# A ring of six buffers with exponents a batch ahead, and the last multiplication of each weight unit on GpSimd

## What is computed

```python
x = x + mlstm(layernorm(x), ctx, ctx, Wi, bi, Wf, bf, ln_scale)   # 16 heads of 32
x = x + ffn(layernorm(x), w_gate, w_up, w_down)                   # 512 -> 2048 -> 512
# mlstm, per batch and head, s = 256:
log_D = where(ltr, fcum_i - fcum_j, -inf) + ig_j
D     = exp(log_D - rowmax(log_D))
C     = (q @ k.T / sqrt(32)) * D
h     = (C / (max(|C.sum(-1)|, exp(-rowmax)) + 1e-6)) @ v          # then layernorm per head, scaled
# ffn: every operand is quantized in blocks of 32 along its last axis
mx_linear(x, w) = q_act(x) @ q_w(w).T
out   = mx_linear(silu(mx_linear(x, w_gate)) * mx_linear(x, w_up), w_down)
```

## Time and profile before

| | us |
|---|---|
| median of 3 runs | 636.48 |
| lowest and highest | 633.6 and 640.59 |
| the profiled execution, its own time | 635.27 |
| its span, first to last instruction | 633.5 |
| busy: TensorE, VectorE, ScalarE, GpSimd | 519.4, 453.5, 247.2, 208.0 |
| mean granted TensorE clock, share of full | 0.732 |

### The profile page before, as it was taken

The page is one execution under the profiler, slowest core; times in us unless marked ns, Lnnn a source line. Parts: engine busy times, 40 slices in busy tenths (PEclk is TensorE's granted clock), DMA queues, the critical chain, the costliest instruction groups (busy, mean ns, idle before and its releaser), DMA issues.

```text
span 633.5 us, 10373 instructions
## 1 busy us (share of the span) xinstructions
PE 519.4 (82%) x3465; PEld 355.1 (56%) x3465; DVE 453.5 (72%) x639; ACT 247.2 (39%) x343; POOL 208.0 (33%) x207
## 2 busy tenths in 40 slices
PE   2699984989859698597895986855999999999994
PEld 2599973767646466475574764622444444444441
DVE  3899995566657867578566775469788888888781
ACT  1566642242324425233334342242443343344331
POOL 3222001101515316152171331435434444443542
PEclk9966855575557657555565565677999999999998
DMA  6654414111221402214032020201011121020010
GB/s 198 210 205 147 128 58 128 57 55 50 73 65 34 138 21 82 67 34 137 0 100 70 1 67 0 67 0 66 2 57 43 33 66 34 33 66 33 33 66 33
DMA packets 30564, 43.70 MB, mean 69 GB/s; under 512 B 6980, under 2 KB 11972, under 8 KB 30532
## 3 DMA queue, kind: packets, MB, share of 16 engines
q1 hardware_dynamic: 30532, 43.26, 21.4%
HBM read 34.41 MB, written 8.85 MB: 68 GB/s over the span
## 4 chain that ended last, share of the span: by engine, by line
PE 36%; DVE 32%; issue 18%; POOL 8%; ACT 4%; DMA 1%; DVEq 1%; POOLq 1%; SPq 0%; ACTq 0%
PE psA L1256 10%; PE psA L1330 5%; PE psA L1339 5%; POOL kTa L666 5%; PE psB L1247 3%; DVE qTa L1112 3%; DVE kTa L1103 3%; DVE pam L917 3%; PE psC L1213 3%; DVE wq L943 3%; DVE wy L940 3%; PE psB L1245 2%; DVE wam L917 2%; DVE wm L935 2%; PE psB L1349 2%
## 5 line engine op out<-in xcount | busy, mean ns | idle before, releaser
L1256 PE MATMUL psA<-vp,CT 128*128 128x33 f32 x512 | 107.2, 370 | 50.0 <-DVE CT L1016 49.9
L1256 PEld LDWEIGHTS psA<-vp,CT 128*128 128x128 f32 x512 | 100.5, 293 | 68.4 <-issue 64.3
L1016 DVE SCALAR_TENSOR_TENSOR CT<-psA,Dt 128x512 f32<-128x512 f32 x64 | 42.7, 688 | 95.4 <-ACT Dt L793 87.8
L666 POOL TENSOR_TENSOR kTa<-kTa,ps 128x1024 bf16<-128x1024 bf16 x32 | 61.2, 1913 | 103.7 <-DVE kTa L1115 103.7
L793 ACT ACTIVATE Dt<-psB 128x512 f32<-128x512 f32 x64 | 37.3, 594 | 91.4 <-PE psB L1247 91.4
L1330 PE MATMUL psA<-WgT,qTa 128*128 128x512 bf16 x256 | 65.2, 401 | 7.4 <-ACT qTa L821 4.3
L1357 PE MATMUL psC<-WdT,kTa 128*128 128x512 bf16 x256 | 61.9, 386 | 2.4 <-ACT kTa L869 2.4
L1339 PE MATMUL psA<-WuT,qTa 128*128 128x512 bf16 x256 | 60.9, 381 | 0.0
L869 ACT ACTIVATE kTa<-psB 128x1024 bf16<-128x1024 bf16 x32 | 32.8, 1024 | 55.2 <-PE psB L1349 54.7
L1103 DVE TENSOR_TENSOR kTa<-kTa,psA 128x1024 f32<-128x1024 f32 x32 | 39.0, 1220 | 18.7 <-PE psA L1339 18.5
L713 ACT ACTIVATE wm<-wm,wbase 128x1024 f32<-128x1024 f32 x24 | 27.6, 1149 | 58.5 <-DVE wm L935 58.5
(11 more groups left out here) (131 smaller groups left out, 923.5 us busy)
## 6 DMA issues: line engine op xcount, KB each, us to landing
early<-in_x_dram SPq DMA_DIRECT2D x16, 512.0 KB, 4.1
early<-in_ctx_dram SPq DMA_DIRECT2D x8, 512.0 KB, 4.6
wraw<-in_L_ffn_w_down_dram SPq DMA_DIRECT2D x8, 512.0 KB, 5.9
...
```

The costliest lines, as they stand in the source:

```text
L666: nc.gpsimd.tensor_tensor(blocks(pd[h]), blocks(pc[h]), spread(ps4[h][:, :], PB), ALU.mult).then_inc(pq_ready.sem, 1)
L1016: nc.vector.scalar_tensor_tensor(out=CT[n % HPC][:, :], in0=psA[:, n % HPC, :], scalar=float(DH) ** -0.5, in1=Dt[n % 2][:, :], op0=ALU.mul ...
L1256: last = nc.tensor.matmul(psA[:, j, i4 * VW:(i4 + 1) * VW], CT[n % HPC][:, i4 * P:(i4 + 1) * P], vp[p][:, c, HPC * i4 + j, :], start=i4 == ...
```

## The change

- `Dt` (2 buffers) and `CT` (4) become one ring `DC` of 6. `c_mult` writes its product over the exponents that it read, so `exps` no longer waits for `c_ready`, nor `c_mult` for `h_done`.
- Decay and `exps` 0 to 3 of batch b + 1 run at the end of step b; `centre(b, 1)`, `copy_v(b, 1)`, `state(b)` and `copy_state(b)` move from step b - 1 into step b. TensorE starts a step with a `w_transpose`, then heads 0 to 3 with nothing between them. ScalarE runs `x1_norm` ahead of `copy_h(b, 1)`, and `round_const(2b + B + 3, 1)` stays last.
- `w_back` moves from VectorE to GpSimd, in the preparation and in the steps. In a step GpSimd runs `head_rsqrt`, `residual`, `carry_q`, `w_back`, `x1_rsqrt`, `w_back`, `weigh`, `back_x`. Two waits are added on VectorE: `w_front` waits for the `w_back` of two units before (it overwrites `ws4`), `w_pow` for the `w_round` of the unit before.
- SyncE issues `load_carry(b + 1)` ahead of the wait for `state_mm` and of `load_ctc(b + 1)`.

The diff, cut to its core (what is left out renames the buffers, deletes `w_back` from VectorE's list and brings the first batch's order in line):

```diff
@@ -179,17 +180,16 @@
         Sst = [sb(f"Sst{p}", [P, HC, VW]) for p in range(2)]
         vp = [sb(f"vp{p}", [P, NCH, NH, VW]) for p in range(2)]
         vw = sb("vw", [P, NH, VW])
-        Dt = [sb(f"Dt{n}", [P, HC * P]) for n in range(2)]
-        CT = [sb(f"CT{n}", [P, HC * P]) for n in range(HPC)]
+        DC = [sb(f"DC{n}", [P, HC * P]) for n in range(DCN)]
         hf = [sb(f"hf{p}", [P, NCH, NH, VW]) for p in range(2)]
...
@@ -485,12 +485,12 @@
                 sp.wait_ge(d_mm.sem, d_mm.at(b, 1))
                 settle(sp)
                 load_decay(b + 1, 1 - p)
+                sp.wait_ge(qs_ready.sem, qs_ready.at(b, 1))
+                settle(sp)
+                load_carry(b + 1)
                 sp.wait_ge(state_mm.sem, state_mm.at(b, 1))
                 settle(sp)
                 load_ctc(b + 1)
-                sp.wait_ge(qs_ready.sem, qs_ready.at(b, 1))
-                settle(sp)
-                load_carry(b + 1)
                 if weights:
                     sp.wait_ge(y_ready.sem, y_ready.unit(2 * b + B + 2))
                     settle(sp)
...
@@ -552,6 +552,12 @@
                 chain.link(nc.gpsimd.tensor_scalar(tmp, src, 1.0, LN_EPS, ALU.mult, ALU.add))
                 chain.link(nc.gpsimd.tensor_tensor(dst, tmp, mhalf[:, 0:NCH], ALU.pow))
                 return nc.gpsimd.tensor_tensor(bias, negmean, dst, ALU.mult)
+
+            def w_back(w, p):
+                gp.wait_ge(wn_ready.sem, wn_ready.unit(w))
+                settle(gp)
+                nc.gpsimd.tensor_tensor(blocks(wq[p][:, :]), blocks(wq[p][:, :]), spread(ws4[p][:, :], UB),
+                                        ALU.mult).then_inc(wq_ready.sem, 1)
 
             def x_rsqrt(b):
                 gp.wait_ge(mv_ready.sem, mv_ready.at(b, 1))
...
@@ -584,6 +590,8 @@
             def pre_step(b, p, n, first, last):
                 if not last:
                     x_rsqrt(b + 1)
+                if not first:
+                    w_back(b - 1, 1 - p)
 
             x_rsqrt(0)
             tables()
...
@@ -647,14 +655,19 @@
                 if not first:
                     residual(b - 1)
                 if not last:
+                    carry_q(b + 1, 1 - p)
+                w_back(2 * b + B + 1, 1)
+                if not first:
+                    x1_rsqrt(b - 1)
+                if not last:
+                    w_back(2 * b + B + 2, 0)
                     weigh(b + 1, 1 - p)
-                    carry_q(b + 1, 1 - p)
-                if not first:
-                    x1_rsqrt(b - 1)
                 if not first:
                     back_x(b - 1)
 
+            w_back(B - 1, 1)
             weigh(0, 0)
+            w_back(B, 0)
             carry_q(0, 0)
             pipeline(ch, gp, step)
 
...
@@ -788,9 +800,8 @@
                                      ACT.Copy, scale=float(DH) ** -0.5).then_inc(state_ev.sem, 1)
 
             def exps(b, n):
-                act.wait_ge(c_ready.sem, c_ready.at(b, max(n - 1, 0)))
                 act.wait_ge(d_mm.sem, d_mm.at(b, n + 1))
-                nc.scalar.activation(Dt[n % 2][:, :], psB[n % 2][:, :], ACT.Exp).then_inc(d_exp.sem, 1)
+                nc.scalar.activation(DC[n % DCN][:, :], psB[n % 2][:, :], ACT.Exp).then_inc(d_exp.sem, 1)
 
             def copy_h(b, p, c):
                 if c == 0 and not (isinstance(b, int) and b < 2):
...
@@ -821,38 +832,37 @@
                 nc.scalar.activation(spent_b[:, b, 0:NCH * E], psC[1][:, :].bitcast(BF16), ACT.Copy).then_inc(xqT_ev.sem, 1)
 
             def step(b, p, n, first, last):
-                exps(b, 0)
-                exps(b, 1)
-                exps(b, 2)
-                exps(b, 3)
+                evac_gate_up(2 * b + B, 0, b)
+                if not first:
+                    head_power(b - 1)
+                copy_h(b, p, 0)
                 exps(b, 4)
-                copy_h(b, p, 0)
                 exps(b, 5)
-                if not first:
-                    head_power(b - 1)
-                if not last:
-                    copy_v(b + 1, 1 - p, 0)
-                evac_gate_up(2 * b + B, 0, b)
+                copy_v(b, p, 1)
                 if not first and not (isinstance(b, int) and b == 1):
                     evac_xq(b - 2)
-                if not last:
-                    copy_v(b + 1, 1 - p, 1)
+                copy_state(b, p)
                 exps(b, 6)
                 exps(b, 7)
                 if not last:
                     round_const(2 * b + B + 2, 0)
+                if not first:
+                    x1_norm(b - 1)
                 copy_h(b, p, 1)
-                if not first:
-                    x1_norm(b - 1)
+                evac_gate_up(2 * b + B + 1, 1, b)
+                if not last:
+                    exps(b + 1, 0)
+                    exps(b + 1, 1)
+                    copy_v(b + 1, 1 - p, 0)
+                    exps(b + 1, 2)
+                    exps(b + 1, 3)
                 square(b, p)
                 if not last:
-                    copy_state(b + 1, 1 - p)
-                evac_gate_up(2 * b + B + 1, 1, b)
-                if not last:
                     round_const(2 * b + B + 3, 1)
 
-            copy_state(0, 0)
             round_const(B + 1, 1)
+            for k in range(HPC):
+                exps(0, k)
             pipeline2(ch, act, step)
             head_power(B - 1)
 
...
@@ -925,6 +935,7 @@
             def w_front(w, p, n):
                 ve.wait_ge(w_ld[p], 16 * n + 16)
                 ch.link(reduce_blocks(blocks(wraw[p][:, :]), wam[p][:, :]))
+                ve.wait_ge(wq_ready.sem, wq_ready.unit_before(w, 2))
                 ch.link(power(wam[p][:, :], ws4[p][:, :]))
                 ch.link(inverse(ws4[p][:, :], winv[p][:, :], INV_W))
                 nc.vector.tensor_tensor(blocks(wy[p][:, :]), blocks(wraw[p][:, :]), spread(winv[p][:, :], UB),
...
@@ -932,6 +943,7 @@
 
             def w_pow(w, p):
                 ve.wait_ge(y_ready.sem, y_ready.unit(w))
+                ve.wait_ge(wn_ready.sem, wn_ready.unit_before(w, 1))
                 nc.vector.tensor_scalar(wm[:, :].bitcast(I32), wy[p][:, :].bitcast(I32), EXPO, None,
                                         ALU.bitwise_and).then_inc(pow_ready.sem, 1)
 
...
@@ -1004,17 +1009,15 @@
                                     ALU.subtract).then_inc(split_ready, 1)
 
             w_round(B, 0)
-            w_back(B, 0)
             w_pow(B + 1, 1)
 
             ch = Chain(ve, dve_step, 2 * DVE_LINKS)
 
             def c_mult(b, n):
                 ve.wait_ge(qk_done.sem, qk_done.at(b, n + 1))
-                ve.wait_ge(h_done.sem, h_done.at(b, max(n - HPC + 1, 0)))
                 ve.wait_ge(d_exp.sem, d_exp.at(b, n + 1))
-                nc.vector.scalar_tensor_tensor(out=CT[n % HPC][:, :], in0=psA[:, n % HPC, :], scalar=float(DH) ** -0.5,
-                                               in1=Dt[n % 2][:, :], op0=ALU.mult, op1=ALU.mult).then_inc(c_ready.sem, 1)
+                nc.vector.scalar_tensor_tensor(out=DC[n % DCN][:, :], in0=psA[:, n % HPC, :], scalar=float(DH) ** -0.5,
+                                               in1=DC[n % DCN][:, :], op0=ALU.mult, op1=ALU.mult).then_inc(c_ready.sem, 1)
 
             def head_var(b, p):
                 n = hf[p][:, :, :, DH]
...
@@ -1074,7 +1077,6 @@
                 w_round(2 * b + B + 1, 1)
                 if not first:
                     head_norm(b - 1, 1 - p)
-                w_back(2 * b + B + 1, 1)
                 for k in range(HPC, 2 * HPC):
                     c_mult(b, k)
                 if not last:
...
@@ -1084,7 +1086,6 @@
                 if not last:
                     w_front(2 * b + B + 3, 1, b + B // 2 + 1)
                     w_round(2 * b + B + 2, 0)
-                    w_back(2 * b + B + 2, 0)
                 if not first:
                     x1_round(b - 1)
                 if not last:
...
@@ -1274,51 +1275,50 @@
                     last = nc.tensor.transpose(dst[:, k * P:(k + 1) * P], xd[:, k * P:(k + 1) * P], identb[:, :])
                 last.then_inc(xqT_mm.sem, 1)
 
+            def decay_qk(b, p):
+                decay(b, p, 0)
+                qk(b, 0)
+                decay(b, p, 1)
+
             def step(b, p, n, first, last):
+                w_transpose(2 * b + B, 0, rows_order)
                 for k in range(HPC):
                     heads(b, p, k)
-                    decay(b, p, k + 2)
-                if not last:
-                    centre(b + 1, 0)
+                decay(b, p, 4)
+                decay(b, p, 5)
+                centre(b, 1)
                 qk(b, 1)
-                w_transpose(2 * b + B, 0, rows_order)
                 if b >= 2:
                     pe.wait_ge(wT_ev.sem, wT_ev.unit(2 * b + B))
                     x_transpose(b - 2)
-                if not last:
-                    centre(b + 1, 1)
-                heads(b, p, 4)
+                state(b)
                 decay(b, p, 6)
-                heads(b, p, 5)
                 decay(b, p, 7)
```

(21 more changed lines are left out.)

26 lines of the change are left out of this document (10 added, 16 removed).

## The result

The changed kernel takes 567.06 us (median of 4 runs, 564.68 to 572.07) against 635.04 for the kernel before (4 runs). The ratio is 0.8947, interval 0.890 to 0.899: 68 us less, where 584 had been forecast and 562 to 609 given as the range. The profiled execution took 566.52 us, its span is 564.7 against 633.5. Some kernels have executions over 1.5% longer than their fastest; the ratios here leave these out and the medians take them in, and the profiles of e2, e7 and e10 fell on such a one.

The account below looks back on a forecast made before the run. A loop of about 25 us of TensorE's list, 13.5 of VectorE's and 2.6 of handing over bounds the attention steps. 635.3 less 49.9 (six steps), 1 (ends) and 0 (preparation) gives 584 us, range 562 to 609.

Parts of the forecast that it names:

- rival B: Attention steps: TensorE at the upper clock level throughout, so VectorE bounds at 29.0 us a step; 560 us total, chance 0.09.
- A full step: Attention step on TensorE: 35.8 of work less 5.5 for the clock plus 2 of waiting, 32.3 us.
- the clock term: TensorE's time at the upper clock level in a step: 5.5 us taken, bounds 3.3 and 10.3.
- The ends of the stage: Attention stage's ends: +3.2 ahead of heads(0, 0), -3 in step 0, -1 in the last step; together -1 us.
- `w_back` off VectorE: Attention steps: two w_back of 1.22 us leave VectorE's list; port lock costs 0 to 3.8 a step, 1 taken.
- The added waits: Attention steps: w_front waits 0 to 1 us, w_pow nothing, TensorE for copy_h 0 to 3, 2 taken.
- The preparation: Before the attention steps: eight w_back leave VectorE but TensorE doesn't get shorter; 0 us, bounds -1.5 and +1.5.
- The signs: New profile: steps of 31 to 34 us, c_mult right behind w_pow, TensorE waiting for hf, clock 0.55 to 0.65.
- A: Attention steps: clock stays as it is, waits at their bounds, 35.5 us a step; 604 us total, chance 0.2.
- D: Attention steps: VectorE and GpSimd exclude each other throughout, 45.3 us a step; slower at 663 us, chance 0.04.
- E: Attention steps: exps still last in the loop, only 2.4 + 1 us a step go; 615 us, chance 0.03.
- C: Attention steps: next exponents late, copy_h(b, 1) held another 4 us, 36.3 us a step; 608 us total, chance 0.08.

Follow-up runs that it names:

- e2: Kernel before with every w_back moved to GpSimd, nothing else changed; 626.55 us, ratio 0.986.
- e7: Changed kernel with copy_h(b, 1) ahead of x1_norm and eight added matmuls, results unused, ahead of heads 0; 560.90 us, ratio 0.882.
- e10: Changed kernel with copy_h first, x1_round behind c_mult 0 to 3 of a later step and eight matmuls added before heads 0; 570.41 us, ratio 0.895.
- e1: Changed kernel with every w_back back on VectorE, ring and early exponents kept; 574.45 us, ratio 0.906.
- e8: Kernel before with the ring of six buffers and without the waits for c_ready and h_done, all orders kept; 632.98 us, ratio 0.996.
- e5: Changed kernel with the w_back of the preparation (7 of its 8) on VectorE again; 567.70 us, ratio 0.899.
- e4: Changed kernel with copy_h(b, 1) ahead of x1_norm(b - 1) on ScalarE; 569.85 us, ratio 0.897.
- e12: Repeat run: changed kernel with copy_h(b, 1) ahead of x1_norm and eight added matmuls ahead of heads 0; 563.26 us, ratio 0.881.

## Why the prediction was right, point by point

*The time.* The measured 567.06 lies within 562 to 609, but 17 us below the 584 that was forecast and 7 below the band of 574 to 594 that was given 0.56. It is nearer rival B's 560 than the forecast, though B's mechanism didn't come. So the range was met with 5 us to spare, and that is partly luck: four terms erred the same way, by 9.5 us in the steps, 6.2 at the ends of the stage, 1.7 in the preparation and 0.5 in the rest.

*What bounds the kernel.* Right. The loop through TensorE, VectorE's tail and the exponents behind `round_const` was the place of the gain: e1 shows 60 us from ring, order and SyncE's list together, e8 none that is clear from the buffers alone. SyncE's new order was not tried by itself; no engine waits for `load_ctc` or a weight load in the attention steps of the changed kernel's profile.

*A full step: 32.3 forecast, 30.7 measured.* The sum was 35.8 less 5.5 at the upper clock plus 2 of waiting. Measured: a clock share of 0.62 over 30.7 us is 7.4 us at the upper level, and TensorE's idle is (184.29 - 174.96) / 6 = 1.6. That gives 35.8 - 7.4 + 1.6 = 30.0, within 0.7 of the step. So the form of the sum holds; the clock term was 1.9 us too small and the wait 0.4 too large. The bounds for the clock (3.3 to 10.3) held; the value between them was a guess. Over six steps this is 59.4 gained against 49.9.

*The ends of the stage: -1 forecast.* Here is the largest term that was mis-sized in proportion. For `heads(0, 0)`'s place and step 0 the sum was near, but both terms were off: decay 0 to `heads(0, 0)` grew by 2.0 us and not 3.2 (102.94 to 109.74, before 104.64 to 109.41), and step 0 went from 32.26 to 31.53 and not to 29.3, as its clock share of 0.55 is 3.2 us at the upper level where 5.5 had been put. Together that is +1.3 against the forecast's +0.2. The last step's term was far off. From `heads(7, 0)` to the first feed-forward matmul it was 31.6 us and is 23.0. TensorE's timeline and the windows view of the last step in the changed kernel, then the timeline in the kernel before:

```profile
325.56 6.98 PE L1257 MATMUL psA<-vp,DC 128*128 128x33 f32 x32
...
345.56 1.04 PE L1182 MATMUL psC<-identb,wq 128*128 128x128 bf16 x8
348.61 2.99 PE L1330 MATMUL psA<-WgT,qTa 128*128 128x512 bf16 x7 [2.00 <-issue]
```

```profile
325.40:347.00 21.60, 21.20 (x196) 17.66 (x193) 11.00 (x19) 9.85 (x17) 11.44 (x12) 0.66 0.15 49
```

```profile
412.86 1.03 PE L1181 MATMUL psC<-identb,wq 128*128 128x128 bf16 x8
416.96 3.29 PE L1330 MATMUL psA<-WgT,qTa 128*128 128x512 bf16 x8 [3.07 <-issue]
```

Of these 8.5 us, 7.5 lie ahead of the last transpose (27.5 us from `heads(7, 0)` before, 20.0 after), and 1.0 behind it, where the evacuation no longer stands behind `square` in ScalarE's list, which I had not counted. Of the 7.5, 1.7 are idle (2.1 before, 0.4 now); the clock share went from 0.56 to 0.66, which is 3.3 against some 6.9 us at the upper level: another 3.6. The wait for `copy_h` of 1 us that I had set against them did not come. Another 1.0 is the transpose that now opens a step and so lies ahead of `heads(7, 0)`. The other 1.2 us are left unexplained.

*`w_back` off VectorE.* The forecast took 1 us of lock a step (a choice between 0 and 3.8); steps 1 to 6 have 157.16 us of VectorE busy, 26.2 each, against 27.4 - 2.5 = 24.9 before without `w_back`: 1.3. Its value was not written down as a figure of its own; e1 and e2 give 7 and 9 us.

*The added waits.* `w_front`'s wait 0 to 1: 1.8 us over steps 1 to 6, 0.3 a step. `copy_h`'s 0 to 3, taken 2: 1.2. But e4 shows that this term was no true cost: without it VectorE's tail sets the step, so the forecast's VectorE path of 31 was the second bound, as near to 30.7 as TensorE's.

*The preparation.* 0 forecast, and e5's time agrees; the profiled execution has 1.7 us less there, within what executions differ by. But the medians over all profiles lie 4.4 us apart (104.3 and 108.7), more than the 2 us that were named as the sign of being wrong, so this term is not settled.

*The signs.* No idle time ahead of `heads(b, 0)`, `c_mult` right behind `w_pow`, a wait for `hf` ahead of `qk(b + 1, 0)` and a clock of 0.62 came as named. Steps of 31 to 34 us did not: they alternate between 29.7 and 31.7, mean 30.7. Steps under 30 us were named as the sign of a wrong clock term, and three of the six are.

*The rivals.* A, D and E did not happen: no step is near 35, and e2, the move without the new order, is at 626.55. C's chain is real and short. B, VectorE as the bound at a high clock, was priced at 29.0 a step; e4 and e12 come nearest, at 31.1 and 30.1. What it left out is the wait for `qk` and for the exponents of pieces 6 and 7 between c_mult 3 and 7, 2.6 and 1.2 us at 276.76 and 279.22 above.
